# Second normalisation of a gated cross-attention and mixture-of-experts block: scale and bias on ScalarE in place of a two-scalar operation on VectorE

## The chip, the cores and the metric

The kernel runs on one core of a Trainium2 chip. The metric is the time of one execution on the device in microseconds (us). Timed runs give a median; one more execution was recorded by the hardware profiler, and every row below comes from that recording. Engines are named as the profile names them: PE is TensorE (PEld its weight loads), DVE is VectorE, ACT is ScalarE, POOL is GpSimd, SP is SyncE, which here only issues DMAs; SPq, POOLq and so on are the engines' queues.

## The reference: what is computed

There are four sequences (B = 4) of 512 tokens with 512 channels. Each passes a gated cross-attention and then a gated feed-forward part that is a mixture of eight experts (two per token) plus one shared expert:

```python
x = x + jnp.tanh(g_xattn[0]) * xattn(_layernorm(x), ctx_512, Wq, Wkv_expand, Wout)
x = x + jnp.tanh(g_ffn[0])   * ffn(_layernorm(x), gate_w, w1, w2, w3, ws1, ws2, ws3)

def _layernorm(x, axis=-1, eps=1e-05):
    m = jnp.mean(x, axis=axis, keepdims=True)
    v = jnp.var(x, axis=axis, keepdims=True)
    return (x - m) / jnp.sqrt(v + eps)

# ffn: scores = softmax(xf @ gate_w.T); top 2 of 8 experts; y = weighted sum of the
# two chosen experts' outputs; z = silu(xf @ ws1.T) * (xf @ ws3.T) @ ws2.T; y + z
```

The second `_layernorm`, the one ahead of the feed-forward part, is what the change is about.

## The kernel before, in words

The kernel is one program with an instruction list for each engine, written out by hand. Nothing is scheduled by a tool: each engine executes its own list in order, and engines wait for each other on semaphores. A block is one sequence, b = 0 to 3, of four tiles of 128 tokens.

**Blocks.** `iteration(b, prev, nxt)` exists on every engine. It runs the attention of block b, interleaved with `feed_forward(prev)`, the shared expert and the router of the block before. Block 0 is written out, blocks 1 and 2 are a hardware loop, and block 3 (`nxt` false) is written out again. `last_feed_forward` then does the shared expert and the router of block 3. After it comes the expert part: 39 tiles of gathered token rows through the experts' weights, with sums scattered back to the output. That part can begin only when all tokens are routed.

**Products in two halves.** Each f32 operand of a product is held as two f16 parts. ScalarE writes the high part (`turn_hi` for transposed tiles, line 541), VectorE the low part (`turn_lo`, line 815, or 816), and TensorE multiplies three pairs.

**From attention to feed-forward.** For each tile i of block b, VectorE does `make_x1` (line 863, the residual sum into `x_sb`) and `statistics2` (line 831). After tiles 0 and 1, and again after tiles 2 and 3, it does `aggregate2` for the pair p = 0 or 1 (lines 838 and 842, the variance), GpSimd does `power2` (line 415, the inverse root into column 2 of `ln2`), and VectorE does `norm2(b, p)` (line 885): two instructions, each subtracting the mean and multiplying by the inverse root, from `x_sb` into `xn2`. TensorE transposes `xn2` (`turn_x2`, line 1298), ScalarE and VectorE make the halves `x2T`, and `hidden` (line 1343) and `router` use them. SyncE stores `xn2` rows to `xrows` for the expert part.

**Where the two pairs stand.** Pair 0 is normalised at the end of `iteration(b)`, pair 1 at the beginning of the next feed-forward, in `after_attention(f)`. On ScalarE, the places that matter are the end of `iteration` (the scores' copies `scores_out`, line 598, and the softmax's `exps`, line 603; in block 3 instead `split_piece(3)` to `split_piece(7)`), and the beginning of `feed_forward` and `last_feed_forward` (two `turn_hi`, then `exps` or `split_piece(8)`, then `tanh_h`, line 607).

**Weights.** From block 2 on, the eight experts' weights come in 16 pieces. `split_piece(k)` on ScalarE (line 541, 128x1536) writes the high half of piece k and, for pieces whose low half GpSimd makes, a scaled copy back; the low half is then made by GpSimd (line 462, four instructions a piece) or VectorE (line 816). GpSimd's other work is the softmax's subtraction and multiplication (lines 446, 453) and the scatters of token lists (line 432).

The first normalisation already has the form scale and bias on ScalarE: `norm1` (line 573) with `bias1` (line 857) on VectorE.

Of the kernel before, what the change touches and what calls it, by code (L numbers as in the profile page):

```python
# [25 lines left out]
ALU = mybir.AluOpType  # L26
# [44 lines left out]
def block_program(nc, x, ctx_rows, gates, wq, wkv, wout, gate_w, experts, out):  # L71
    with ExitStack() as stack:  # L72
# [129 lines left out]
        y_mm, x1_ready = sem("y_mm"), sem("x1_ready")  # L202
        ln2_step, ln2_stats, xn2_ready = sem("ln2_step"), sem("ln2_stats"), sem("xn2_ready")
        lg_mm, lg_max, lg_out, lg_exp = sem("lg_mm"), sem("lg_max"), sem("lg_out"), sem("lg_exp")
        route_step, mask_ready, pos_mm, route2_step, pos_out, pairs_ready = (sem(n) for n in (
# [333 lines left out]
        def _(act):  # L539
# [60 lines left out]
            def exps(b, i):  # L600
                act.wait_ge(sub_ready, 4 * b + i + 1)
                si = S[:, i * NH * SK:(i + 1) * NH * SK]
                nc.scalar.activation(si, si, ACT.Exp, scale=float(HD) ** -0.5 / (S_Q * S_KV)).then_inc(exp_ready, 1)

            def tanh_h(b, i):
                act.wait_ge(h_mm, 4 * b + i + 1)
                nc.scalar.activation(th[:, i % 2, :], mm_bank[i % 2][:, 0:INTER], ACT.Tanh,
                                     scale=0.5 / (S_LN * S_W)).then_inc(th_ready, 1)
# [14 lines left out]
            def feed_forward(f, nxt):  # L623
# [10 lines left out]
                scores_out(c, 3)  # L634
                turn_hi(c, "x2", 1)
                exps(c, 2)
                tanh_h(f, 0)
# [32 lines left out]
            def last_feed_forward(f):  # L670

                c = f + 1
                turn_hi(c, "x2", 0)
                turn_hi(c, "x2", 1)
                split_piece(8)
                tanh_h(f, 0)
# [21 lines left out]
            def iteration(b, prev, nxt):  # L698
# [22 lines left out]
                if nxt:  # L721
                    scores_out(b + 1, 0)
                    scores_out(b + 1, 1)
                    exps(b + 1, 0)
                    scores_out(b + 1, 2)
                    exps(b + 1, 1)
                else:
                    for k in range(3, 8):
                        split_piece(k)
# [80 lines left out]
        def _(dve):  # L810
# [68 lines left out]

            def norm2(b, p):  # L880
                if not isinstance(b, int) or b > 0:
                    dve.wait_ge(st_rows, 64 * b)
                dve.wait_ge(ln2_power, 2 * b + p + 1)
                for i in (2 * p, 2 * p + 1):
                    V.tensor_scalar(xn2[:, i * D:(i + 1) * D], x_tile(4 * b + i), ln2[:, i, 0:1], ln2[:, i, 2:3],
                                    ALU.subtract, ALU.mult).then_inc(xn2_ready, 1)

# [145 lines left out]
            def after_attention(f):  # L1033
# [6 lines left out]
                turn_lo(c, "x2", 1)  # L1040
                norm2(f, 1)

# [128 lines left out]
            def iteration(b, prev, nxt):  # L1171
# [41 lines left out]
                aggregate2(b, 0)  # L1213
                norm2(b, 0)
                if nxt:
# [410 lines left out]
```

## Time and profile before

| | |
|---|---|
| median of 3 timed runs | 522.28 us (520.1 to 526.24) |
| profiled execution, its own time | 521.47 us |
| span of the profiled execution | 519.7 us |
| mean granted TensorE clock | 0.947 of full speed |
| PE busy | 436.1 us (84%) |
| DVE busy | 318.6 us (61%) |
| ACT busy | 245.8 us (47%) |
| POOL busy | 245.0 us (47%) |

The execution's own time has 1.77 us around the span. Times inside the span are counted from its start. An engine's busy share is an average over stages: the start to about 72 us, four blocks of 56 to 63 us each, the last feed-forward to about 301 us, a gap in which lists and rows are fetched, and the expert part from 316 us. In a timeline row the first number is the start, the second the length from the first start to the last end when several instructions are merged (x2), and the square bracket says how long the engine had been idle before it and what it had waited for.

### The profile page before, as it was taken

The page shows a single profiled execution, that of the slowest core. Times are in us where ns is not written, and L with a number is a line of the kernel's source. Part 1 is how long each engine was busy: PE and PEld are TensorE (multiplying, and loading weights), DVE is VectorE, ACT ScalarE, POOL GpSimd, SP SyncE. Part 2 cuts the span into 40 slices and gives each one's busy share as a digit, 9 for nine tenths or more (in the row PEclk, how much of TensorE's full clock was granted, in tenths as well). Part 3 has the DMA queues.
Part 4 walks back from the last instruction along what each step waited for, and adds up shares of the span by engine and source line. Part 5 has one row for each costly group of instructions (what it writes and reads, how often), then busy time and mean ns, then how long its engine had stood idle before and what let it go on. Part 6 is the DMA issues. An engine that isn't in the chain of part 4 may idle for free. (4 is left out here: it accounts for less than half of the span.)

```text
span 519.7 us, 8145 instructions
## 1 busy us (share of the span) xinstructions
PE 436.1 (84%) x2432; PEld 232.6 (45%) x2433; DVE 318.6 (61%) x641; ACT 245.8 (47%) x425; POOL 245.0 (47%) x209
## 2 busy tenths in 40 slices
PE   2699599988999889987867625999999999999991
PEld 1355355554555545553333202455455545445540
DVE  4798868987588865897988761433433334343330
ACT  4878644663356534485746320343344343434430
POOL 4008325405544154465687813255555555455432
PEclk9999989999999999998978855999999999999997
DMA  8970001120011100325747664266576575655653
GB/s 327 412 304 1 0 1 42 42 81 2 1 64 38 61 0 0 108 116 182 244 121 241 165 122 102 41 109 113 104 121 109 99 119 102 123 105 110 108 75 42
DMA packets 26375, 55.31 MB, mean 106 GB/s; under 512 B 9136, under 2 KB 9264, under 8 KB 25712
## 3 DMA queue, kind: packets, MB, share of 16 engines
q0 software_dynamic: 9760, 20.49, 22.3%
q1 hardware_dynamic: 16592, 34.54, 20.2%
q8 instruction: 11, 0.18, 0.1%
q14 instruction: 12, 0.10, 0.1%
HBM read 31.51 MB, written 23.50 MB: 106 GB/s over the span
## 5 line engine op out<-in xcount | busy, mean ns | idle before, releaser
L1293 PE MATMUL bank<-arena 128*128 128x512 f16 (+1 forms) x576 | 109.5, 347 | 3.2 <-issue 1.5
L1293 PE MATMUL bank<-arena,GT 128*128 x468 | 109.6, 385 | 0.1
L526 POOL DMA_INDIRECT out<-Y,entry x39 | 61.6, 1579 | 84.4 <-ACT Y L792 39.0
L1293 PE MATMUL bank<-arena,gT 128*128 (+1 forms) x330 | 84.1, 393 | 6.3 <-DVE gT L815 5.8
L1293 PEld LDWEIGHTS bank<-arena 128*128 128x128 f16 x576 | 55.9, 98 | 51.4 <-issue 3.8
L541 ACT ACTIVATE arena<-bank 128x512 f16<-128x512 f32 (+1 forms) x88 | 49.7, 586 | 52.5 <-PE bank L1293 32.3
L1293 PEld LDWEIGHTS bank<-arena,GT 128*128 128x128 f16 x468 | 46.3, 99 | 48.5 <-issue 3.1
L815 DVE TENSOR_TENSOR GT<-bank,GT 128x512 f16<-128x512 f32 x39 | 27.0, 692 | 61.0 <-ACT GT L541 61.0
L453 POOL TENSOR_TENSOR arena<-arena,rd 128x1024 f32<-128x1024 f32 x16 | 30.5, 1905 | 52.3 <-DVE rd L928 52.3
L1293 PEld LDWEIGHTS bank<-arena,gT 128*128 128x128 f16 x330 | 32.7, 100 | 44.7 <-DVE gT L815 5.8
L1293 PE MATMUL bank<-arena,x2T 128*128 128x512 f16 x192 | 47.9, 403 | 4.4 <-DVE x2T L815 4.4
L509 POOL DMA_INDIRECT G<-xrows,entry x39 | 38.8, 996 | 26.5 <-issue 12.6
L1257 DVE SCALAR_TENSOR_TENSOR uu<-th,bank 128x256 f32<-128x256 f32 x39 | 16.4, 421 | 56.3 <-ACT th L777 56.3
L777 ACT ACTIVATE th<-bank 128x256 f32<-128x256 f32 x39 | 15.0, 384 | 69.8 <-PE bank L1293 69.8
L792 ACT ACTIVATE Y<-bank,entry 128x512 f32<-128x512 f32 x39 | 26.8, 688 | 44.7 <-PE bank L1293 44.7
L446 POOL TENSOR_TENSOR arena<-arena,mx 128x1024 f32<-128x1024 f32 x16 | 30.3, 1899 | 26.4 <-DVE mx L917 26.4
L1298 PE MATMUL bank<-ident,G 128*128 128x128 f32 x156 | 25.1, 285 | 19.6 <-DMA G<-xrows,entry 14.8
L432 POOL DMA_INDIRECT lists<-pair,slot x32 | 34.1, 1065 | 13.9 <-issue 13.9
L1298 PE MATMUL bank<-ident,arena 128*128 128x128 f32 x192 | 29.1, 291 | 13.6 <-DVE arena L815 9.5
L815 DVE TENSOR_TENSOR arena<-bank,arena 128x512 f16<-128x512 f32 x48 | 31.3, 684 | 9.8 <-ACT arena L541 9.2
L816 DVE SCALAR_TENSOR_TENSOR arena<-bank,arena 128x512 f16<-128x512 f32 (+1 forms) x40 | 25.8, 654 | 14.0 <-ACT arena L541 13.7
L462 POOL TENSOR_TENSOR arena<-x_sb,arena 128x384 f16<-128x384 f32 x32 | 30.0, 970 | 7.5 <-ACT x_sb L541 7.5
(126 smaller groups left out, 596.2 us busy)
## 6 DMA issues: line engine op xcount, KB each, us to landing
x_sb<-in_experts SPq DMA_DIRECT2D x16, 768.0 KB, 6.1
xrows<-xn SPq DMA_DIRECT2D x16, 256.0 KB, 2.2
out<-x_sb SPq DMA_DIRECT2D x16, 256.0 KB, 2.1
xrows<-Y SPq DMA_DIRECT2D x1, 2304.0 KB, 23.9
out<-Y SPq DMA_DIRECT2D x1, 2304.0 KB, 28.8
x_sb<-in_x SPq DMA_DIRECT2D x2, 1024.0 KB, 7.8
x_sb<-in_x SPq DMA_DIRECT2D x1, 2048.0 KB, 15.8
arena<-in_wq SPq DMA_DIRECT2D x1, 1024.0 KB, 8.0
```

What stands on the lines that cost most here:

```text
L432: nc.gpsimd.indirect_dma_start(out=lists[:, :], out_offset=bass.IndirectOffsetOnAxis(ap=slot[:, i, k:k + 1], axis=0), in_=pair[:, i, k, :] ...
L446: nc.gpsimd.tensor_tensor(sv, sv, mx[:, i, :].unsqueeze(2).to_broadcast([P, NH, SK]), ALU.subtract).then_inc(sub_ready, 1)
L453: nc.gpsimd.tensor_tensor(sv, sv, rd[:, i, :].unsqueeze(2).to_broadcast([P, NH, SK]), ALU.mult).then_inc(p_ready, 1)
L462: nc.gpsimd.tensor_tensor(wlo[:, cols], raw[:, cols], whi[:, cols], ALU.subtract).then_inc(w_split[w_slot(k)], 1)
L509: nc.gpsimd.indirect_dma_start(out=G[:, j % RING, :], out_offset=None, in_=xrows[:, :], in_offset=bass.IndirectOffsetOnAxis(ap=entry[:, j, ...
L526: nc.gpsimd.indirect_dma_start(out=out, out_offset=bass.IndirectOffsetOnAxis(ap=entry[:, j, 0:1], axis=0), in_=Y[:, j % RING, :], in_offse ...
L541: return nc.scalar.activation(dst, src, ACT.Copy, scale=scale)
L792: nc.scalar.activation(Y[:, s, :], e_y[s][:, :], ACT.Copy, scale=entry[:, bass.ds(j, 1), 1:2].rearrange("p n c -> p (n c)").bitcast(F32)). ...
L815: return V.tensor_tensor(dst, src, high, ALU.subtract)
L816: return V.scalar_tensor_tensor(out=dst, in0=src, scalar=scale, in1=high, op0=ALU.mult, op1=ALU.subtract)
L1293: last = nc.tensor.matmul(dst, a, b, start=n == 0, stop=n == len(steps) - 1)
L1298: last = nc.tensor.transpose(dst[:, c * P:(c + 1) * P], src[:, c * P:(c + 1) * P], ident[:, :])
```

## The change

The second normalisation becomes x times scale plus bias on ScalarE. VectorE no longer touches the 128x512 tiles; it makes one small tensor for each pair of tiles, bias = -mean times inverse root (128x2, into column 3 of `ln2`), behind the same wait for GpSimd's power. The new semaphore `ln2_bias` tells ScalarE of it. On ScalarE, `norm2(b, 0)` stands in the lists of blocks 0 to 2 between `scores_out(b + 1, 2)` and `exps(b + 1, 1)`, and in block 3 between `split_piece(5)` and `split_piece(6)`. `norm2(f, 1)` stands behind the second `turn_hi` in both kinds of feed-forward. No other instruction is added or removed, and the queues of SyncE, GpSimd and TensorE are as before.

```diff
+            def norm2(b, p):
+
+                if not isinstance(b, int) or b > 0:
+                    act.wait_ge(st_rows, 64 * b)
+                act.wait_ge(ln2_bias, 2 * b + p + 1)
+                for i in (2 * p, 2 * p + 1):
+                    if not isinstance(b, int):
+                        pass_waits(act)
+                    nc.scalar.activation(xn2[:, i * D:(i + 1) * D], x_tile(4 * b + i), ACT.Identity,
+                                         bias=ln2[:, i, 3:4], scale=ln2[:, i, 2:3]).then_inc(xn2_ready, 1)
+
...
                 turn_hi(c, "x2", 0)
                 scores_out(c, 3)
                 turn_hi(c, "x2", 1)
+                norm2(f, 1)
                 exps(c, 2)
                 tanh_h(f, 0)
...
                 turn_hi(c, "x2", 0)
                 turn_hi(c, "x2", 1)
+                norm2(f, 1)
                 split_piece(8)
                 tanh_h(f, 0)
...
                     scores_out(b + 1, 2)
+                    norm2(b, 0)
                     exps(b + 1, 1)
                 else:
-                    for k in range(3, 8):
+                    for k in range(3, 6):
+                        split_piece(k)
+                    norm2(b, 0)
+                    for k in range(6, 8):
                         split_piece(k)
...
-            def norm2(b, p):
-                if not isinstance(b, int) or b > 0:
-                    dve.wait_ge(st_rows, 64 * b)
+            def bias2(b, p):
+
+                w = ln2[:, 2 * p:2 * p + 2, :]
                 dve.wait_ge(ln2_power, 2 * b + p + 1)
-                for i in (2 * p, 2 * p + 1):
-                    V.tensor_scalar(xn2[:, i * D:(i + 1) * D], x_tile(4 * b + i), ln2[:, i, 0:1], ln2[:, i, 2:3],
-                                    ALU.subtract, ALU.mult).then_inc(xn2_ready, 1)
+                V.scalar_tensor_tensor(out=w[:, :, 3], in0=w[:, :, 0], scalar=-1.0, in1=w[:, :, 2],
+                                       op0=ALU.mult, op1=ALU.mult).then_inc(ln2_bias, 1)
...
                 turn_lo(c, "x2", 1)
-                norm2(f, 1)
+                bias2(f, 1)
...
                 aggregate2(b, 0)
-                norm2(b, 0)
+                bias2(b, 0)
```

Three places show how ScalarE's list moves. The first is the written-out end of block 3 and the beginning of the last feed-forward: `arena<-bank 128x512 x4` are the attention's high halves, `arena<-x_sb` and `x_sb<-x_sb` the pieces 3 to 7, `x2T<-bank` the two `turn_hi`, the next pair piece 8, `th<-bank` the first tanh. Before:

```order
L541 ACTIVATE arena<-bank 128x512 x4
L541 ACTIVATE arena<-x_sb 128x1536 x2
L541 ACTIVATE x_sb<-x_sb 128x1536
L541 ACTIVATE arena<-x_sb 128x1536 x2
L541 ACTIVATE x_sb<-x_sb 128x1536
L541 ACTIVATE arena<-x_sb 128x1536
L541 ACTIVATE x2T<-bank 128x4x128 x2
L541 ACTIVATE arena<-x_sb 128x1536
L541 ACTIVATE x_sb<-x_sb 128x1536
L607 ACTIVATE th<-bank 128x256
```

The same place on ScalarE, from piece 4 on, in the changed kernel:

```order
L542 ACTIVATE x_sb<-x_sb 128x1536
L542 ACTIVATE arena<-x_sb 128x1536
L614 ACTIVATE xn<-x_sb,ln 128x512 x2
L542 ACTIVATE arena<-x_sb 128x1536
L542 ACTIVATE x_sb<-x_sb 128x1536
L542 ACTIVATE arena<-x_sb 128x1536
L542 ACTIVATE x2T<-bank 128x4x128 x2
L614 ACTIVATE xn<-x_sb,ln 128x512 x2
L542 ACTIVATE arena<-x_sb 128x1536
L542 ACTIVATE x_sb<-x_sb 128x1536
L619 ACTIVATE th<-bank 128x256
```

Pair 0 now stands ahead of both instructions of piece 6 and the one of piece 7, which stand ahead of the two `turn_hi`; pair 1 stands ahead of piece 8 and the tanh.

The second place is ScalarE's end of block 0, where the last rows were a scores copy and the second softmax exponential; now the pair stands between them (in blocks 1 and 2 likewise):

```order
L542 ACTIVATE arena<-bank 128x512 x4
L599 ACTIVATE arena<-bank 128x512 x4
L604 ACTIVATE arena<-arena 128x1024
L599 ACTIVATE arena<-bank 128x512 x2
L614 ACTIVATE xn<-x_sb,ln 128x512 x2
L604 ACTIVATE arena<-arena 128x1024
```

The fifth row is new; the rows around it stood in this order before.

The third is VectorE at the end of block 3, after the changed variance step: one small instruction, then the residual sum of tile 2, its statistics, the low half of transposed tile 0 and the residual sum of tile 3, in the changed kernel:

```order
L860 TENSOR_SCALAR ln<-ln 128x2
L902 SCALAR_TENSOR_TENSOR ln<-ln 128x2
L881 SCALAR_TENSOR_TENSOR x_sb<-bank,gl,x_sb 128x512
L849 BN_STATS mv<-x_sb 128x6
L833 TENSOR_TENSOR x2T<-bank,x2T 128x4x128
L881 SCALAR_TENSOR_TENSOR x_sb<-bank,gl,x_sb 128x512
```

Where the second row stands there were two instructions `xn<-x_sb,ln 128x512` before; nothing else moved on VectorE.

## Rows read from the trace of the kernel before

**Rows 1.** Windows: us, busy (count) of each engine, PEclk, DMA share, GB/s.

```profile
135.00:197.50 62.50, 57.92 (x368) 32.55 (x368) 49.14 (x102) 31.52 (x57) 25.56 (x19) 1.00 0.10 34
254.00:301.00 47.00, 34.43 (x187) 16.23 (x186) 39.60 (x84) 24.84 (x28) 38.20 (x38) 0.81 0.57 166
```

**Rows 2.** Timeline of GpSimd in the last feed-forward.

```profile
259.62 3.51 POOL L462 TENSOR_TENSOR arena<-x_sb,arena 128x384 f16<-128x384 f32 x4
...
285.96 1.03 POOL L432 DMA_INDIRECT lists<-pair,slot  x1 [1.35 <-issue]
```

**Rows 3.** Waits of SyncE's queue, 300 to 310 us: us in total, times, longest.

```profile
SPq L366 <- DMA lists<-pair,slot: 2.6, 1, 2.6
```

**Rows 4.** Timeline of VectorE, end of block 3 and last feed-forward.

```profile
259.42 3.74 DVE L842 TENSOR_SCALAR ln<-ln 128x2 f32<-128x2 f32 x1
264.08 1.00 DVE L885 TENSOR_SCALAR xn<-x_sb,ln 128x512 f32<-128x512 f32 x2 [0.92 <-POOL ln L415]
...
266.50 0.67 DVE L815 TENSOR_TENSOR x2T<-bank,x2T 128x512 f16<-128x512 f32 x1
...
270.19 2.12 DVE L885 TENSOR_SCALAR xn<-x_sb,ln 128x512 f32<-128x512 f32 x2 [0.33 <-POOL ln L415]
...
275.40 1.28 DVE L815 TENSOR_TENSOR x2T<-bank,x2T 128x512 f16<-128x512 f32 x2
```

**Rows 5.** Timeline of ScalarE over the same stretch.

```profile
254.17 2.84 ACT L541 ACTIVATE arena<-x_sb 128x1536 f16<-128x1536 f32 x2
256.92 1.47 ACT L541 ACTIVATE x_sb<-x_sb 128x1536 f32<-128x1536 f32 x1
261.89 1.48 ACT L541 ACTIVATE arena<-x_sb 128x1536 f16<-128x1536 f32 x1 [3.51 <-DMA x_sb<-in_experts]
265.43 1.08 ACT L541 ACTIVATE x2T<-bank 128x512 f16<-128x512 f32 x2 [2.06 <-PE bank L1298]
...
272.57 0.39 ACT L607 ACTIVATE th<-bank 128x256 f32<-128x256 f32 x1 [0.30 <-PE bank L1293]
```

**Rows 6.** Small VectorE operations: one source line, then timeline rows with GpSimd's beside.

```profile
L857 DVE SCALAR_TENSOR_TENSOR ln<-ln x3: 162/168/168, 12.7 to 67.5; 128x4 f32<-128x4 f32 x2, 128x8 f32<-128x8 f32 x1
...
245.65 0.93 DVE L968 SCALAR_TENSOR_TENSOR sc<-oh,sc 128x32 f32<-128x32 f32 x1
...
245.62 3.52 POOL L462 TENSOR_TENSOR arena<-x_sb,arena 128x384 f16<-128x384 f32 x4 [5.36 <-ACT x_sb L541]
```

**Rows 7.** Timeline of VectorE, end of block 1 and next feed-forward, GpSimd's row last.

```profile
144.96 2.59 DVE L885 TENSOR_SCALAR xn<-x_sb,ln 128x512 f32 x2 [0.85 <-POOL ln L415]
...
150.75 0.68 DVE L815 TENSOR_TENSOR x2T<-bank,x2T 128x512 f16<-128x512 f32 x1
...
153.57 1.00 DVE L885 TENSOR_SCALAR xn<-x_sb,ln 128x512 f32 x2 [0.33 <-POOL ln L415]
...
144.91 1.89 POOL L446 TENSOR_TENSOR arena<-arena,mx 128x1024 f32<-128x1024 f32 x1
```

**Rows 8.** Timeline of ScalarE over the same stretch.

```profile
146.84 1.06 ACT L603 ACTIVATE arena<-arena 128x1024 f32<-128x1024 f32 x1 [2.05 <-POOL arena L446]
148.72 0.60 ACT L541 ACTIVATE x2T<-bank 128x512 f16<-128x512 f32 x1 [0.83 <-PE bank L1298]
...
154.28 0.39 ACT L607 ACTIVATE th<-bank 128x256 f32<-128x256 f32 x1 [2.22 <-PE bank L1293]
...
159.47 1.51 ACT L573 ACTIVATE arena<-x_sb,ln 128x512 f32 x2
```

**Rows 9.** Timeline of TensorE: the same stretch, then block 2's transposes of pair 1.

```profile
151.49 2.76 PE L1293 MATMUL bank<-arena,x2T 128*128 128x512 f16 x12 [1.05 <-DVE x2T L815]
...
155.19 2.75 PE L1293 MATMUL bank<-arena,x2T 128*128 128x512 f16 x12
...
217.03 1.11 PE L1298 MATMUL bank<-ident,xn 128*128 128x128 f32 x8 [0.24 <-DVE xn L885]
```

## What the change does to the time: the prediction

> **What bounds the kernel now.** The windows view comes first, by stage [rows 1]. In a steady block PE is busy 57.9 of 62.5 us at full clock, DVE 49.1, ACT 31.5: TensorE sets the pace there and has some 4.6 us of waits, so freeing VectorE can return only what lies in those waits. In the last feed-forward (254 to 301 us) PE is busy 34.4 of 47 us, DVE 39.6, POOL 38.2, and the granted clock is 0.81. There no engine is full and a chain through all of them sets the time: normalise, transpose, halves, router, choice of experts, and then GpSimd's scatters, which begin at 285.96 [rows 2]. The expert part waits for those lists, so what this chain loses, the end loses. The timelines of each engine around the eight normalisations, read side by side, give the rest: each engine works its list in order, so for every place I ask what stands behind the new instruction.
>
> **The pieces, priced.** Removed from VectorE: two instructions for each of eight pairs, 1.00 us a pair when undisturbed [rows 4, 7], but 2.59 when GpSimd's softmax instruction is running (it starts at 144.91, the norm at 144.96) [rows 7]. Added to ScalarE: two activations a pair; the first normalisation's pair of the same shape takes 1.51 [rows 8]. Added to VectorE: the bias, 0.17 us by `bias1`'s 162 to 168 ns [rows 6]. Whether the bias is held up by GpSimd, as the old norm was, no row shows for this very instruction. The nearest is the same operation on small SBUF tensors at 245.65: 0.93 us, started 0.03 after a GpSimd instruction [rows 6]. The bounds are 0 and the length of GpSimd's instruction; I take held, since this row has the bias's kind of operands.
>
> The Trainium skill, Perfetto Trace Analysis, section Optimizing Scalar/DVE Operations, says that an operation with a VectorE performance mode is faster there, and that moving it to ScalarE may pay if VectorE is saturated. The trace agrees with its first half (1.00 against 1.51 a pair); for the second half, VectorE is at 79% in a steady block. Taken as a rule against the change, it would add 0.5 us for each pair on the path and no more.
>
> **Blocks 0 to 2 (steady block 1 as the example).** The bias would start where the norm did, 144.96, right behind GpSimd's 1.89 us instruction from 144.91, and end at about 146.85 instead of 147.55. ScalarE, idle there until 146.84 [rows 8], then does the pair to 148.4, the exponential (1.06) to 149.4 and the `turn_hi` (0.60), which before began at 148.72, to 150.0. VectorE's `turn_lo` then starts at 150.1, not 150.75 [rows 7]; by VectorE's own list, 3.2 us from the norm's end to `turn_lo`, it would be 150.05, so both arrive together. Gain so far 0.65, and `hidden(0)` on PE, which had waited 1.05 for it and began at 151.49 [rows 9], begins at 150.85. For pair 1 the bias starts 0.65 before 153.57, at 152.9, with GpSimd idle (its next work waits for VectorE's `head_max`, queued behind the bias), and ends at 153.1; ScalarE's pair ends at 154.6, where VectorE's ended at 154.57. So the transpose of tile 3 and `hidden(1)`, 155.19 before, move by 0.1 at most: the gain is given back, because the slower pair starts earlier and ends at the same time. Behind it ScalarE's exponential and tanh are late: tanh at 155.5, not 154.28 [rows 8], and the two `turn_hi` of tiles 2 and 3 by 1.0. TensorE works on `hidden(1)` until 157.9, and VectorE gets through its queue by 158.0, so this is covered. Result: -0.1 for each of blocks 0 and 1. In block 2 PE did wait 0.24 for VectorE's norm ahead of this pair's transposes [rows 9], so an earlier pair 1 is worth more; there I take -0.4. Sum -0.6; bounds per block -0.65 (nothing given back) and +1.0 (the late `turn_hi` uncovered).
>
> **Block 3, pair 0.** This is the costly place. Piece 5 on ScalarE ends at about 255.6 (half of the pair from 254.17) [rows 5]. Now ScalarE waits there for the bias. The bias needs GpSimd's power, which stands behind its `split_piece(4)`, busy until 263.13 [rows 2]; the norm began at 264.08 [rows 4]. So ScalarE stands for 8.7 us, with pieces 6 and 7 queued behind. Before, these filled that wait: piece 6 until 258.4, piece 7 from 261.89 to 263.37 when its load had landed [rows 5]. Now: bias to 264.25, pair 264.3 to 265.8, piece 6 (1.42 + 1.47, less overlap: 2.8) to 268.5, piece 7 (1.4) to 269.9, and only then `turn_hi` of tile 0, which had begun at 265.43: +4.5. VectorE had come to `turn_lo` of tile 0 at 266.50; the half is now ready at 270.5: +4.0. Behind it on VectorE stand the residual sum of tile 3, its statistics and the variance, so all of pair 1 moves by 4.0.
>
> **Block 3, pair 1.** The bias would start at 270.19 + 4.0 = 274.2. GpSimd's next work is `split_piece(6)`, ready by then, so the bias is held by its first instruction. The norm there took 2.12 against 1.00, a hold of 1.1 [rows 4]; the small operation at 245.65 was held 0.7 [rows 6]. I take 0.8 all told, to 275.0. The upper bound is `L842`, which stood through all four of GpSimd's instructions (3.74 us) [rows 2, 4]. Then the pair to 276.5, piece 8 (2.8, by piece 6) to 279.3, and tanh of tile 0 at 279.3, not 272.57 [rows 5]: +6.7. VectorE had not used the tanh at once: its two `hidden` steps (0.8) ended at 275.4 where `turn_lo` of tiles 2 and 3 began [rows 4], so they began 1.65 after the tanh's end. Now they follow directly: 279.7 + 0.8 = 280.5, +5.1. The router needs that low half of tile 3. From here the chain has the spacing of before: logits, choice, places, scatters, landing, list loads, gather. The late pieces have cover: loads 10 to 15 are each released by splits that move by no more than the chain.
>
> **The sum.** +5.1 in block 3, -0.6 in the others: +4.5. Against the profiled execution's own time, 521.47 + 4.5 = 526.0. That execution lies 0.8 below the median of the timed runs, so I name the time from the median: 522.28 + 4.5 = **526.8 us**. Since the bound for telling a change is about 1% (5.2 us), and the three runs spread from 520.1 to 526.24, this is just within it.
>
> **Rivals.** (B) The bias is so short that GpSimd's instruction doesn't hold it. Then in a block it ends at 145.15, `hidden(0)` is limited by PE's own transposes (about -1.0), and ScalarE's pair 1 ends 0.5 earlier: -0.6, -0.6, -0.9; and block 3 is 0.8 cheaper. +4.3 - 2.1 = +2.2, 524.5. Against it speaks the row at 245.65. (C) Not all of the delay reaches the end. SyncE waited 2.6 us for the last scattered packets to land, after it had issued the last store [rows 3]. Should the stragglers not recur at the new instant, the end has 2.6 less: +1.9, 524.2. For it: every other wait in this tail is of an engine; against it: the stores and the load that share the queues with the scatters move along. (D) The bias of block 3's pair 1 is held through all four of GpSimd's instructions, as `L842` was: 3.5 in place of 0.8, +7.2, 529.5. For it: the same place in GpSimd's list (four in a row, nothing between); against it: the norm that stood in this very place was held by one. The same time results if the late `turn_hi` in the blocks have no cover (+1.0 a block). (E) The other side, **faster**: VectorE bounds the steady blocks, and what it is relieved of comes off in full. It is 3.59 - 0.34 = 3.25 us a block for an unheld bias, -9.7 for three, with block 3 net -4.6, 517.7. It decides from 1.7 a block (5.1 / 3). By the skill's page named above, moving the work pays where VectorE is saturated. Against it: VectorE is idle 13.4 of 62.5 us in a block, and its lead runs into products that are not ready [rows 1].
>
> **How the numbers follow.** Forecast 0.52, B 0.12, C 0.12, D 0.14, E 0.08, anything else 0.02. The range that leaves out E and little of D, with the forecast's own bounds (525.0 to 528.8), is 523.0 to 530.0. Slower by over 1% (over 527.5): nearly all of D and a third of the forecast, 0.31. Faster by over 1% (under 517.1): half of E and the rest, 0.06. Within 1%: 0.63.
>
> **What would show it.** In the changed kernel's trace: ScalarE idle for 8 to 9 us ahead of the first activation into `xn` in block 3, waiting for the bias (the central step); the `turn_hi` of tile 0 there 4 to 5 us later against the start of the block's first residual sum; the scatters of block 3 about 4.5 later than 285.96 in the span's time. In the blocks: bias instructions of 1.9 us for pair 0 and 0.17 for pair 1; the start-to-start spacing of blocks (62.5 us) shorter by about 0.1. The prediction is wrong if that spacing falls by more than 0.5, if the bias of pair 0 is short, or if SyncE's wait for the last scattered packets, 2.6 us before, is gone.

## The result, and the profile after

The changed kernel takes 527.57 us (median of 20 runs, 524.0 to 531.32) beside 525.05 us (20 runs, 519.83 to 528.72) for the kernel before on the same chips: a ratio of 1.0073 with a 95% interval of 1.0045 to 1.0101, so 3.8 us slower (2.4 to 5.3). The time is inside the predicted range. Ratios, here and below, leave out executions over 1.5% above the fastest of their kernel, which are two of e4's twelve (525.63 and 526.80 us; its median below still counts them) and one of the kernel before. The profiled execution has a span of 524.9 us against 519.7. Below, a time "into the block" counts from the start of that block's first residual sum (`make_x1`).

The page's first lines, busy time of each engine:

```profile
span 524.9 us, 8171 instructions
...
PE 434.5 (83%) x2432; PEld 231.1 (44%) x2433; DVE 309.5 (59%) x633; ACT 255.3 (49%) x441; POOL 244.7 (47%) x209
```

VectorE lost 9.1 us of work, ScalarE gained 9.5, and the kernel became slower. The same two windows as in [rows 1]:

```profile
135.00:197.50 62.50, 57.11 (x364) 32.01 (x362) 47.74 (x99) 33.29 (x60) 25.59 (x19) 1.00 0.09 34
254.00:301.00 47.00, 31.38 (x174) 14.62 (x171) 31.08 (x77) 25.85 (x31) 33.94 (x35) 0.79 0.58 166
```

In the last feed-forward every engine but ScalarE does less in 47 us than before (VectorE 31.1 against 39.6: two normalised pairs are gone, the variance step took 0.62 for 3.74, and later work has moved out of the window). The stretch is longer, not fuller. The new ScalarE line and the new VectorE line, by source line:

```profile
L614 ACT ACTIVATE xn<-x_sb,ln x16: 801/809/817, 82.9 to 273.3; 128x512 f32<-128x512 f32 x8, 128x512 f32 x8
...
its engine sat idle before it (us, times) until:
  DVE ln L902: 21.9, 8
```

```profile
L902 DVE SCALAR_TENSOR_TENSOR ln<-ln x8: 164/522/1869, 81.0 to 271.6; 128x2 f32<-128x2 f32 x8
```

ScalarE stood idle for 21.9 us in front of its normalising activations, waiting for the eight biases. Such a wait costs only where something late is queued behind it, and the experiments below show that this is block 3. ScalarE there, to be read beside [rows 5]:

```profile
254.17 1.47 ACT L542 ACTIVATE arena<-x_sb 128x1536 f16<-128x1536 f32 x1
261.86 1.52 ACT L614 ACTIVATE xn<-x_sb,ln 128x512 f32<-128x512 f32 x2 [6.22 <-DVE ln L902]
263.29 1.47 ACT L542 ACTIVATE arena<-x_sb 128x1536 f16<-128x1536 f32 x1
264.66 1.47 ACT L542 ACTIVATE x_sb<-x_sb 128x1536 f32<-128x1536 f32 x1
266.04 1.47 ACT L542 ACTIVATE arena<-x_sb 128x1536 f16<-128x1536 f32 x1
267.41 1.06 ACT L542 ACTIVATE x2T<-bank 128x512 f16<-128x512 f32 x2
272.62 1.52 ACT L614 ACTIVATE xn<-x_sb,ln 128x512 f32<-128x512 f32 x2 [4.16 <-DVE ln L902]
274.05 1.47 ACT L542 ACTIVATE arena<-x_sb 128x1536 f16<-128x1536 f32 x1
275.42 1.47 ACT L542 ACTIVATE x_sb<-x_sb 128x1536 f32<-128x1536 f32 x1
276.80 0.37 ACT L619 ACTIVATE th<-bank 128x256 f32<-128x256 f32 x1
```

Pieces 6 and 7 (263.29 to 267.4) run behind the pair, with the two `turn_hi` straight behind them; piece 8 (274.05) and the tanh follow pair 1 in the same way. VectorE, to be read beside [rows 4]:

```profile
255.74 1.76 DVE L834 SCALAR_TENSOR_TENSOR arena<-x_sb,arena 128x1536 f16<-128x1536 f32 x1 [2.04 <-ACT arena L542]
257.41 0.74 DVE L881 SCALAR_TENSOR_TENSOR x_sb<-bank,gl,x_sb 128x512 f32<-128x512 f32 x1
...
259.42 0.62 DVE L860 TENSOR_SCALAR ln<-ln 128x2 f32<-128x2 f32 x1
261.60 0.16 DVE L902 SCALAR_TENSOR_TENSOR ln<-ln 128x2 f32<-128x2 f32 x1 [1.56 <-POOL ln L416]
...
268.02 0.69 DVE L833 TENSOR_TENSOR x2T<-bank,x2T 128x512 f16<-128x512 f32 x1 [4.75 <-ACT x2T L542]
...
271.65 0.88 DVE L902 SCALAR_TENSOR_TENSOR ln<-ln 128x2 f32<-128x2 f32 x1 [0.25 <-POOL ln L416]
...
277.99 1.28 DVE L833 TENSOR_TENSOR x2T<-bank,x2T 128x512 f16<-128x512 f32 x2
```

VectorE, relieved of the normalisation, waits 4.75 us for ScalarE's high half. GpSimd's timeline there, where the power of pair 0 now comes at 260.84 (before: behind its split from 259.62, [rows 2]) and the scatters of block 3 at 288.56 (before 285.96):

```profile
256.67 4.21 POOL L463 TENSOR_TENSOR arena<-x_sb,arena 128x384 f16<-128x384 f32 x4
260.84 0.73 POOL L416 TENSOR_TENSOR ln<-ln,minus_half 128x2 f32<-128x2 f32 x1
...
288.56 1.03 POOL L433 DMA_INDIRECT lists<-pair,slot  x1 [1.35 <-issue]
```

And SyncE's wait for the last scattered packets, 2.6 in [rows 3]:

```profile
SPq L367 <- DMA lists<-pair,slot: 4.9, 1, 4.9
```

The difference of the spans, 5.2 us, put together from the traces' milestones (us; "first residual sum" is `make_x1` of tile 0):

| stretch | before | after | difference |
|---|---|---|---|
| start to block 0's first residual sum | 75.30 | 74.13 | -1.17 |
| to block 3's first residual sum | 178.85 | 177.98 | -0.87 |
| tile 0's to tile 1's residual sum, block 3 | 3.26 | 5.30 | +2.04 |
| to the first scatter of block 3 | 28.55 | 31.15 | +2.60 |
| to the last scatter | 9.91 | 9.93 | +0.02 |
| to the first load of a list | 12.18 | 14.49 | +2.31 |
| to the first gather | 4.32 | 3.76 | -0.56 |
| to the end of the span | 207.33 | 208.16 | +0.83 |

The first row lies ahead of the first changed instruction (the bias at 81.0) and differs between executions by as much (74.1 to 76.2 in the kernels below, 78.4 in e4). Rows two to four give +3.77, beside 3.8 in the timed runs, but they aren't the change's work alone, and that they agree so closely is in part chance. Row two holds two things that come and go between profiles of kernels with the same work there: a stop of TensorE of 1.21 us at 197.58, and a fall of TensorE's granted clock that before has in block 2 and after hasn't (1.6 us). Without both it is about -0.4. Row three is block 2's gain given back at a load (3.47 us in e6, which changes block 3 alone, and 5.28 in e7, which doesn't change it). The last rows of the span, +2.31 at the landing above all, are left to the part on rival C.

A steady block's pair 0 and pair 1 in block 1, first on ScalarE, to be read beside [rows 7, 8]:

```profile
145.82 1.52 ACT L614 ACTIVATE xn<-x_sb,ln 128x512 f32 x2 [2.24 <-DVE ln L902]
...
148.20 0.58 ACT L542 ACTIVATE x2T<-bank 128x512 f16<-128x512 f32 x1
...
151.90 1.52 ACT L614 ACTIVATE xn<-x_sb,ln 128x512 f32 x2 [1.68 <-DVE ln L902]
...
154.28 0.36 ACT L619 ACTIVATE th<-bank 128x256 f32<-128x256 f32 x1
```

VectorE's two biases there, the first behind GpSimd's softmax instruction, the second free:

```profile
143.75 1.87 DVE L902 SCALAR_TENSOR_TENSOR ln<-ln 128x2 f32<-128x2 f32 x1 [0.84 <-POOL ln L416]
...
151.51 0.16 DVE L902 SCALAR_TENSOR_TENSOR ln<-ln 128x2 f32<-128x2 f32 x1 [0.19 <-POOL ln L416]
```

TensorE's `hidden(0)` and the transposes ahead of `hidden(1)`, to be read beside [rows 9]:

```profile
149.55 2.76 PE L1310 MATMUL bank<-arena,x2T 128*128 128x512 f16 x12 [0.26 <-DVE x2T L833]
152.77 1.43 PE L1315 MATMUL bank<-ident,xn 128*128 128x128 f32 x8 [0.45 <-ACT xn L614]
154.04 2.32 PE L1310 MATMUL bank<-arena,x2T 128*128 128x512 f16 x10
```

Into the block, `hidden(0)` begins at 12.74 (before 151.49 - 138.02 = 13.47), 0.73 earlier, and `hidden(1)` at 17.23 (before 17.17): the gain is given back within one block. TensorE's wait moved from 1.05 ahead of `hidden(0)` to 0.45 ahead of the last transpose, whose releaser is now ScalarE's pair.

### The profile page after: what moved, and what is told of

It reads as the page before. It is cut to its first block and busy times, and to the rows that moved or that the text cites. A ratio compares the mean times of both kernels' runs of the same rounds, so it can differ in the third digit from the quotient of the medians.

```text
span 524.9 us, 8171 instructions
## 1 busy us (share of the span) xinstructions
PE 434.5 (83%) x2432; PEld 231.1 (44%) x2433; DVE 309.5 (59%) x633; ACT 255.3 (49%) x441; POOL 244.7 (47%) x209
## 3 DMA queue, kind: packets, MB, share of 16 engines
q0 software_dynamic: 9760, 20.49, 21.9%
## 5 line engine op out<-in xcount | busy, mean ns | idle before, releaser
L1310 PE MATMUL bank<-arena,gT 128*128 (+1 forms) x330 | 82.5, 387 | 6.3 <-DVE gT L833 5.8
L1315 PEld LDWEIGHTS bank<-ident,G 128*128 128x128 f32 x156 | 18.8, 145 | 34.9 <-issue 30.9
```

Of the source, the lines that this page charges most:

```text
L1310: last = nc.tensor.matmul(dst, a, b, start=n == 0, stop=n == len(steps) - 1)
L1315: last = nc.tensor.transpose(dst[:, c * P:(c + 1) * P], src[:, c * P:(c + 1) * P], ident[:, :])
```

## The experiments

All eleven kernels carry two small edits beside the one named: GpSimd's loads of the numbers that its adds wait for assert the numbers' bounds, and ahead of the expert part TensorE waits for all pieces of a round where it waited for those of one expert. E1 is the kernel before with these edits alone, e2 the changed kernel with them; every other experiment is to be read against these two. Each was timed in five rounds. The columns are the ratio to the kernel before on the same chip, and three lengths from the profiled execution: from block 0's to block 3's first residual sum, from there to the first scatter of block 3, and SyncE's wait for the last scattered packets.

| kernel | median, us | ratio (95%) | blocks 0-2 | to scatter | landing wait |
|---|---|---|---|---|---|
| before | | | 178.85 | 31.81 | 2.6 |
| after | 527.57 | 1.0073 (1.0045 to 1.0101) | 177.98 | 36.45 | 4.9 |
| e1 before | 520.72 | 0.9973 (0.9950 to 0.9996) | 180.49 | 31.36 | 2.5 |
| e2 after | 527.33 | 1.0097 (1.0064 to 1.0131) | 178.01 | 36.48 | 3.4 |
| e3 pair 0 behind pieces | 523.30 | 1.0012 (0.9986 to 1.0038) | 181.14 | 33.54 | 2.1 |
| e4 both behind pieces | 521.40 | 0.9964 (0.9929 to 0.9999) | | | |
| e5 blocks 0-2 only | 522.82 | 1.0001 (0.9970 to 1.0032) | 177.89 | 32.46 | 4.3 |
| e6 block 3 only | 526.73 | 1.0074 (1.0037 to 1.0111) | 178.77 | 36.98 | 4.4 |
| e7 pair 0 of 0-2 only | 519.39 | 0.9937 (0.9901 to 0.9973) | 174.55 | 31.42 | 4.3 |
| e8 e4, stores first | 522.48 | 1.0000 (0.9970 to 1.0029) | 176.99 | 32.90 | 4.0 |
| e9 e1, stores first | 522.44 | 0.9985 (0.9949 to 1.0020) | 178.87 | 32.14 | 3.8 |
| e10 e7, stores first | 519.35 | 0.9927 (0.9896 to 0.9959) | 176.03 | 32.15 | 5.2 |
| e11 pair 0 of all | 521.63 | 0.9972 (0.9938 to 1.0006) | 174.61 | 33.26 | 6.0 |

E4's lengths are left out of the table: its profiled execution took 525.63 us, 4.2 more than its median. In the profiles of after and of e1 to e4, TensorE stands still once at the end of block 1, for 1.2 us (after, e2, e4), 1.9 (e1) and 2.6 (e3); in those of before and of e5 to e11 it doesn't. Kernels with the normalisation on either engine are on both sides, so it isn't the change; what causes it isn't shown. In e3 the granted clock fell behind that stop (0.57 from 200 to 204 us, 1.00 there in e1). So block 1 was longer than before's 62.56 by 1.1 us in after, e2 and e4, by 1.8 in e1 and by 4.3 in e3, which the fourth column includes. As the level of "VectorE everywhere" I take the mean of e1 and e9, 0.9979. E1 to e4 ran on one chip, e5 to e8 on a second and e9 to e11 on a third, so e5 to e8 have no such kernel on their own chip.

**E1 and e2, the two controls.** E1's edit to the waits, in short (that to the bounds is left out here):

```diff
-pe.wait_ge(w_split[w_slot(k)], PARTS * (w_round(k) - 1) + (e + 2) // E * PARTS)
+pe.wait_ge(w_split[w_slot(k)], PARTS * w_round(k))
```

> The kernel before, with the two small edits that every kernel of this study carries: GpSimd's queue asserts the bounds of the value that each add of rows waits for, and TensorE waits for all of the last four weight pieces ahead of the first expert product, in place of a wait that depends on the tile's expert. It is the zero point of the others. Both theories: the pieces were ready 7 us before that product, and GpSimd waits for others in the expert part, so +0.0 us against the kernel before, within 1.0. More than +2 would mean that the assertion is on the path, and then the others are to be read against this one.

> The changed kernel with the same two edits. Both theories: +3.8 us against the kernel before (2.4 to 5.3), and as much against e1. In its trace ScalarE idles about 6 us ahead of the first normalising activation of block 3.

Measured: 0.9973 and 1.0097. The loss by the change is 6.2 us against the mean of e1 and e9 (0.0118 of 522.4), more than the 3.8 of the unedited pair, though the intervals overlap. Against e1 alone, the comparison that was forecast, it is 6.5 us where 3.8 was expected. E1 itself came out 1.4 us below the kernel before, where 0.0 within 1.0 was expected. All comparisons below are among kernels with the edits.

**E5 and e6, one part of the change each.** A selector sends a pair to ScalarE or leaves it on VectorE; in e5 all blocks but block 3 use ScalarE, in e6 block 3 alone.

```diff
+def by_scalar(b, p):
+    return not (isinstance(b, int) and b == B - 1)   # e5
+    return isinstance(b, int) and b == B - 1         # e6
```

> Scale and bias on ScalarE for blocks 0 to 2 only; both pairs of block 3 are normalised by VectorE as before. Theory Q (all of the loss is ScalarE's queue in block 3): no loss; from the residual sum of block 2 to that of block 3 it is 2 us shorter than in e1, as in e2 (51.6 for 53.4), but tile 1 of block 3 waits for weight pieces 4 and 5, so that at most 0.7 arrives: -0.7 to 0 us against e1. Rival S (ScalarE's late exponential and tanh cost in the blocks): +1 to +3 against e1.

> Scale and bias on ScalarE for block 3 only; blocks 0 to 2 are normalised by VectorE as before. Theory Q, as the prediction's own term for block 3: ScalarE waits 8.5 us ahead of pair 0, the scatters of block 3 start 4 to 5 us later from the block's first residual sum, +5 us against e1. Rival S: +3 or less.

Measured: 1.0001 and 1.0074. Against 0.9979 the blocks cost +0.0022 and block 3 +0.0095, together 0.0117, where e2 shows 0.0118. Each ratio is uncertain by some 0.3%, so the parts add up within that, and the loss is block 3's (+5.0 us). E5 missed its expectation, -0.7 to 0 us against e1: it is 1.5 us above e1 and 1.2 above 0.9979, by its number within the rival's +1 to +3. The times don't decide, since the intervals overlap. The trace speaks against the rival: from block 0's first residual sum to block 3's first scatter e5 has 210.35 us, where e9 has 211.01.

ScalarE in e6:

```profile
264.96 1.52 ACT L620 ACTIVATE xn<-x_sb,ln 128x512 f32<-128x512 f32 x2 [8.62 <-DVE ln L918]
...
270.51 1.05 ACT L547 ACTIVATE x2T<-bank 128x512 f16<-128x512 f32 x2
275.71 1.52 ACT L620 ACTIVATE xn<-x_sb,ln 128x512 f32<-128x512 f32 x2 [4.15 <-DVE ln L918]
...
279.88 0.36 ACT L625 ACTIVATE th<-bank 128x256 f32<-128x256 f32 x1
```

With blocks 0 to 2 as before, ScalarE stands idle for 8.62 us. Into the block (which begins at 254.65) the `turn_hi` comes at 15.86, before at 11.28 (+4.6); the tanh at 25.23, before at 18.42 (+6.8); the first scatter at 36.98, before at 31.81 (+5.2).

**E3 and e4, the same work at another place in ScalarE's list.**

```diff
 else:
-    for k in range(3, 6):
-        split_piece(k)
-    norm2(b, 0)
-    for k in range(6, 8):
+    for k in range(3, 8):
         split_piece(k)
+    norm2(b, 0)
```

and in e4 also, in `last_feed_forward`:

```diff
-norm2(f, 1)
 split_piece(8)
+norm2(f, 1)
 tanh_h(f, 0)
```

> The changed kernel with one thing moved: on ScalarE in block 3, the normalisation of pair 0 stands behind pieces 6 and 7 and not ahead of them. Theory Q (the loss is ScalarE's queue in block 3: pieces 6 and 7 held behind the wait for the bias): the pieces fill the wait again, turn_hi of tile 0 is back at the time of before or 0.5 earlier, pair 1 still costs up to 0.1 at the router, so 0 to +1 us against e1, some 3 less than e2. Theory R (the loss is elsewhere: in the landing of the scattered lists and the expert part, or in the blocks): the same as e2, +3.8.

> As e3, and in the last feed-forward pair 1's normalisation stands behind piece 8 on ScalarE, not ahead of it. Theory Q: piece 8 fills the wait for pair 1's bias as well, tanh of tile 0 comes at most 0.8 us later than before, which VectorE had not waited for, and the last low half comes 0.8 earlier: the scatters of block 3 start 0.5 to 1 us earlier than in e1, and the time is -1 to 0 us against e1. Theory R: as e2, +3.8.

Measured: 1.0012 and 0.9964, against 1.0097 with pair 0 ahead of pieces 6 and 7. The same instructions on the same engine, two pieces further down in its list, give back 4.4 us, of which 2.9 can be seen in the trace ahead of the first scatter (33.54 for 36.48). So most of the loss was not the price of ScalarE's pair but of what stood behind its wait. E3 is still 2.0 us above e1, where 0 to 1 was expected; its clock fall in block 1 is one possible reason, and whether the timed runs had it isn't known.

That pair 1 behind piece 8 gives back more isn't shown. By the ratios e4 has 2.5 us less than e3, but the intervals overlap, and e8, which keeps e4's order, is timed at 1.0000. In e4's own profile the first scatter comes 33.61 us into block 3, as in e3. What e4 and e8 do show is that with both pairs behind the pieces no loss is left that could be measured.

In e3 the pieces run through, and nothing waits for pair 0's bias:

```profile
260.67 1.49 ACT L541 ACTIVATE arena<-x_sb 128x1536 f16<-128x1536 f32 x1 [0.89 <-DMA x_sb<-in_experts]
...
265.56 1.49 ACT L541 ACTIVATE arena<-x_sb 128x1536 f16<-128x1536 f32 x1 [2.03 <-DMA x_sb<-in_experts]
266.95 1.51 ACT L613 ACTIVATE xn<-x_sb,ln 128x512 f32<-128x512 f32 x2
268.55 0.60 ACT L541 ACTIVATE x2T<-bank 128x512 f16<-128x512 f32 x1
```

**E7, only the pair that gains.** Pair 0 of blocks 0 to 2 on ScalarE, pair 1 and block 3 on VectorE:

```diff
 def by_scalar(b, p):
-    return not (isinstance(b, int) and b == B - 1)
+    return p == 0 and not (isinstance(b, int) and b == B - 1)
```

> In blocks 0 to 2, pair 0 on ScalarE and pair 1 on VectorE as before; block 3 on VectorE. Theory G (in a block, the gain of 0.6 at the first hidden product is given back because ScalarE's pair 1 takes 1.5 us where VectorE's takes 1.0, with the exponential behind it): the second hidden product keeps the gain, the blocks are 0.5 to 0.7 shorter start to start than in e1 and e5, -1.5 us against e1. Rival: the spacing of the blocks is set elsewhere, and it reads as e5.

Measured: 0.9937, 1.9 us less than e1. The spacings of the blocks' first residual sums are 61.88, 61.79 and 50.88 us, where the kernel before has 62.72, 62.56 and 53.57; of the last difference, 2.69, some 1.3 to 1.6 is the clock (see block 2 below). In block 1 VectorE's pair 1 comes earlier and TensorE has no wait left ahead of `hidden(1)`:

```profile
150.76 2.76 PE L1326 MATMUL bank<-arena,x2T 128*128 128x512 f16 x12 [0.29 <-DVE x2T L839]
153.45 1.19 PE L1331 MATMUL bank<-ident,xn 128*128 128x128 f32 x8
154.47 2.75 PE L1326 MATMUL bank<-arena,x2T 128*128 128x512 f16 x12
```

The gain of 0.7 us at `hidden(0)` is kept: 0.8 a block. E7 and e5 differ in blocks 0 to 2 in pair 1 alone, and e5's first spacing is 62.65: this is the direct evidence that pair 1 on ScalarE gave the gain back.

**E11, pair 0 of all four blocks, in block 3 behind the pieces.**

```diff
 def by_scalar(b, p):
-    return p == 0 and not (isinstance(b, int) and b == B - 1)
+    return p == 0
```

> Pair 0 of all four blocks on ScalarE, in block 3 behind pieces 3 to 7; pair 1 of all on VectorE. Against the kernel with pair 0 of blocks 0 to 2 alone at 0.9937, block 3's pair 0 costs 0.5 us more by ScalarE's longer pair, and VectorE is free for the residual sum of tile 2 one us earlier, which has to wait for TensorE anyhow: 0.994 to 0.996. If ScalarE's list is at all late there (turn_hi behind the pair), up to 1.5 us more: 0.997. If instead it is VectorE that block 3's chain waits for, as its 3.7 us held variance step may hint, it gains 1 us: 0.992.

Measured: 0.9972, and 1.8 us more to the first scatter than e7 (33.26 against 31.42). By its number it fits the middle case of the expectation, but the trace gives only part of it to ScalarE's list: pair 0 starts 0.44 us after its bias has ended, behind piece 7, and takes 0.5 longer than on VectorE, while GpSimd's power had come 1.07 later into the block than in e7 (9.77 for 8.70). In time e11 isn't told apart from e7, since the intervals overlap.

**E8, e9 and e10, the place of a load.** In the traces of after, e2, e3, e5 and e7, tile 1's residual sum in block 3 comes 5.3 to 5.5 us after tile 0's, before 3.3. In the rows of after above, VectorE's split at 255.74 waits 2.04 for ScalarE, and ScalarE waited 2.07 us at 251.40 for the load of a weight piece, which SyncE issues when block 2's stores to the output base have landed. These three kernels let the stores go ahead of the load of the fourth piece:

```diff
-load_pieces(2, 4)
+load_pieces(2, 3)
 store_base(B - 2, 1, PER)
+load_pieces(3, 4)
```

> As e4, and SyncE issues block 2's last three base stores ahead of the load of weight piece 3, not behind it. In e4 the residual sum of tile 1 in block 3 came 5.3 us after that of tile 0, in e1 4.0: it waits for piece 5, whose load waits for these stores to land. Theory D (the 1.9 us that the blocks gain are given back at this load): the stores land 2 to 3 us earlier, tile 1 follows at 3.3 to 4 us, and 1 to 2 us arrive at the end, -1.5 us against e4. Rival: tile 1 waits for something else, no change against e4, or piece 3 itself is now late, +1.

> The kernel before (VectorE's norms everywhere) with SyncE's list changed in one place: block 2's last stores to the output base stand ahead of the load of the fourth weight piece. If the 1.9 to 2.0 us by which tile 1's residual sum of block 3 comes later after a quicker block 2 hangs on that load's place in the queue, this kernel has the first residual sums of block 3 at most 3.3 us apart as before and changes nothing else: 0 to -1 us. If the place of the stores is worth something by itself (the scatters' tail), it shows here as well: -1 to -3 us. Rival: the four loads queued behind then come later and the split of the fourth piece with them: +1 to +2 us.

> Pair 0 of blocks 0 to 2 on ScalarE, everything else on VectorE, and the base stores ahead of the load of the fourth piece. The same kernel without the reordered stores was 0.9937 of before. If the load of pieces behind those stores takes part of block 2's gain, this one keeps it: 1 to 1.5 us less than that kernel, 0.991. If the distance between the residual sums is set otherwise, no difference from 0.994.

Measured: the two residual sums are 3.69, 3.60 and 3.59 us apart in e8, e9 and e10 (e7, without the reordering, 5.28), so the link with the load is real. ScalarE's wait for that load in e8:

```profile
249.46 1.48 ACT L542 ACTIVATE arena<-x_sb 128x1536 f16<-128x1536 f32 x1 [0.45 <-DMA x_sb<-in_experts]
```

But in time it brings nothing: 1.0000 against e4's 0.9964 (1.5 us less had been expected), 0.9985 against e1's 0.9973 (0 to 1 us less expected), 0.9927 against e7's 0.9937, with overlapping intervals in each pair. In e10 the way from block 3's first residual sum to its first scatter isn't shorter than in e7 (32.15 against 31.42). The theory that this distance costs the end its 2 us has fallen. The traces show what ends last there instead. GpSimd in e10:

```profile
254.38 2.20 POOL L440 DMA_INDIRECT lists<-pair,slot  x1 [0.31 <-issue]
...
257.86 3.51 POOL L470 TENSOR_TENSOR arena<-x_sb,arena 128x384 f16<-128x384 f32 x4
261.48 0.73 POOL L423 TENSOR_TENSOR ln<-ln,minus_half 128x2 f32<-128x2 f32 x1
```

The normalisation of pair 0 waits for the power at 261.48, which is 9.41 us into the block; in e7 it comes at 8.70. Tile 1 is earlier in e10, but GpSimd isn't: one of block 2's scatters took 2.20 us beside VectorE's split of 1.76 us that had started at 253.98 (0.96 in e7, where it had started first), and the four split instructions and the power stand behind it.

**Which version is best.** E7 and e10 are both below the kernel before by more than their intervals (3.3 and 3.8 us). Taken together, 0.9932, against e1 and e9 together, 0.9979, it is 0.5% or 2.5 us, with an uncertainty of some 0.3%. So of the 3.6 us some 2.5 belong to moving pair 0 of blocks 0 to 2. The rest would belong to the edits that all these kernels carry; that these gain 1.1 us isn't shown, since e9's interval includes 1.

## Why the prediction held, point by point

**The time.** Forecast +4.5 us, measured +3.8 (2.4 to 5.3); 526.8 against 527.57, with the kernel before at 525.05 in those runs where its median had been 522.28. That the time itself came within 0.8 us is luck: the starting point was 2.8 too low and the change 0.7 too high. The forecast's own bounds, 525.0 to 528.8, follow from no term that it gives; its bounds per block lead to 525.4 and 530.4.

**The prices of the instructions** held: ScalarE's pair 1.52 for 1.51, VectorE's bias 0.16 when free for 0.17. The choice whether GpSimd holds the bias up came out as taken: 1.87 us for pair 0 (predicted 1.9), 0.88 for pair 1 of block 3 (predicted 0.8). So rival B, a bias too short to be held, is refuted by its own row. Rival D, a bias held through four instructions, is refuted by the 0.88; its second form, late `turn_hi` without cover in the blocks, by the spacing of blocks 0 and 1, 62.68 against 62.72.

**Blocks 0 and 1, -0.1 each.** Spacing -0.04 from block 0 to 1, `hidden(0)` 0.73 earlier (predicted 0.65), `hidden(1)` 0.06 later. E7 confirms by the opposite test that pair 1 on ScalarE gives it back. From block 1 to 2 the spacing is 63.69 against 62.56, by the stop of 1.21 us at 197.58; e5, with the same instructions there and no stop, has 62.54.

**Block 2, -0.4, held, and a clock came on top.** The spacing from block 2 to 3 fell by 1.96 (53.57 to 51.61). The change's own part is where TensorE's 2.35 us wait ends, 34.80 us into the block for 35.17: 0.37 earlier. From there to the end of its next long wait it is 6.67 us in after and 8.27 in before, and this 1.60 isn't the change's own work. TensorE's granted clock, windows of the kernel before and of after:

```profile
234.00:238.00 4.00, 2.25 (x7) 1.11 (x8) 3.13 (x6) 1.76 (x4) 3.60 (x4) 0.70 0.64 187
238.00:242.00 4.00, 4.00 (x25) 2.65 (x23) 1.84 (x3) 1.39 (x3) 2.26 (x3) 0.87 0.35 45
```

```profile
234.00:238.00 4.00, 2.69 (x18) 1.92 (x19) 2.69 (x6) 1.82 (x5) 3.60 (x4) 1.00 0.64 197
238.00:242.00 4.00, 2.14 (x15) 1.24 (x14) 3.89 (x7) 2.92 (x5) 1.83 (x3) 1.00 0.34 31
```

In the kernel before the granted clock fell from 2.4 to 1.2 GHz for part of these windows, and six matmuls at 236.21 took 2.77 us where the same six take 1.46; in after it didn't fall. E1, e6 and e9 (VectorE in block 2) show the fall, after, e2, e3, e4, e5, e7, e8 and e11 don't. E10 shows that this is a thing apart from the normalisation: it has e7's instructions there, the clock fell (0.65 and 0.92 in these windows), and its spacing is 52.32 against e7's 50.88. The same stretch is 8.00 us in e10 and 6.66 in e7. So the fall costs 1.3 to 1.6, and the rest is the predicted 0.4. (E5, at 52.70 without a fall, has tile 1's residual sum of block 2 1.1 us later after tile 0's than before; why isn't shown.) The prediction had no term for the clock: a fall in the kernel after and none in before would have moved the result by as much the other way.

**Block 3, pair 0, +4.5 at `turn_hi`.** E6, where nothing ahead of block 3 differs, shows each number of this step: ScalarE stands 8.62 (predicted 8.7), `turn_hi` +4.6 (4.5). In the changed kernel itself it stood 6.22. There piece 5 ended later into the block, behind the load that piece 4 had waited for (2.07 at 251.40), and the power came a little earlier, 8.73 into the block for 9.1. So `turn_hi` was +4.0 there: 0.6 less than in e6, whose power came at 9.30.

**Block 3, pair 1, +5.1 at the scatters.** E6: tanh +6.8 (predicted 6.7), scatters +5.2. In after: +6.3 and +4.6. The timed runs agree: +5.0 us for e6 against the mean of e1 and e9. E3 confirms the cause for pair 0, the pieces queued behind the wait, by removing it. For pair 1 alone the experiments don't: e4 and e3 aren't told apart.

**The sum.** -0.87 and +4.64 to the first scatter in the traces, where I had -0.6 and +5.1. The -0.87 is made of -0.4 of the change's own, +1.1 of the stop at 197.58 and -1.6 of the clock, so its nearness to -0.6 is luck. The +4.64 is 0.5 below e6's +5.2, by the power that came 0.6 earlier into the block.

**The signs.** Of what the prediction said would show it, `turn_hi` (+4.0), the two lengths of the bias and the spacing of the steady blocks came. ScalarE's idle time of 8 to 9 us came in e6 alone (6.22 in the changed kernel), and the scatters began 2.6 us after 285.96, not 4.5, since the whole profile of after lay 2.0 us ahead at block 3's first residual sum.

**Rival C**, stragglers gone, went the other way: SyncE's landing wait is 4.9, not 0. I had said that the prediction would be wrong if that wait vanished; I hadn't allowed for its growth. Over the twelve profiles without e4 it lies between 2.1 and 6.0. It doesn't follow the change, since e5 and e7, with VectorE in block 3, have 4.3, and it doesn't follow when the scatters come: e7, e10 and e11, which scatter early, have 4.3 to 6.0, but e6 and after, which scatter latest, 4.4 and 4.9. In all twelve SyncE issues its last store 18.4 us after the first scatter of block 3, so the wait is in how long the scatters take to land. A store issued 8.9 us after that first scatter lands late in the same profiles (17.3 us after it in e3, which waits 2.1, and 23.8 in e11, which waits 6.0); that other transfers of this stretch slow both is a rival that no run tests. It can hide a gain or a loss: e11 reaches its first scatter 3.1 us sooner than e9 (207.87 against 211.01, counted from block 0's first residual sum, some 1.3 to 1.6 of it the clock), stands 2.2 us longer for the landing, and is timed 0.7 us faster, which isn't told apart from nothing. What sets the landing wasn't settled.

**Rival E**, VectorE bounds the steady blocks: refuted by e5, in which VectorE is relieved in three blocks and the time is 1.0001. It needed 1.7 us a block. With the bias held at 1.87 and free at 0.16, VectorE was in fact relieved of 1.56 a block (3.59 before), and the most that any kernel got is e7's 0.8. The Trainium skill, Perfetto Trace Analysis, section Optimizing Scalar/DVE Operations, says that moving work to ScalarE may make sense where VectorE is saturated. In a steady block VectorE was busy 79%; no run here shows what a fuller VectorE would make of it.

## What to carry to other kernels

Moving an operation to an idler engine moves its wait as well: price the instructions queued behind that wait on the new engine before the operation itself. Here block 3's two pairs in front of weight pieces, where ScalarE stood 8.6 and 4.2 us, cost 5 us, and behind the pieces the same instructions cost nothing that could be measured. And move only the instances that gain: of eight pairs three were worth it, measured together in e7, those that VectorE did while GpSimd held it up.

## What the runs showed of the hardware

A small VectorE instruction that starts as GpSimd works can last as long as GpSimd's instruction: the 128x2 bias took 1.87 us beside GpSimd's 1.89 and 0.16 alone. It goes the other way too: a scatter of GpSimd took 2.20 us in e10 beside a VectorE split of 1.76 that had started 0.40 ahead of it, and 0.96 in e7, where the scatter had started first.

How long VectorE is held by a series of four GpSimd instructions differs. The variance step (`L842`, in after `L860`) was held 3.74 us in the kernel before, to the end of the whole series, having started 0.20 ahead of it (259.42 and 259.62) [rows 2, 4]; in e6, e8, e9 and e10 it was the same. In after it took 0.62, having started 0.32 into the third instruction, and ended with that one; in e2, e3, e4, e5 and e7 it was the same. The bias of pair 1, started 0.05 into a series' first instruction (271.65 and 271.60), took 0.88, one instruction. But starting inside a series is no protection. In e1 the step started 0.21 into the second of the four and was held to the end of the fourth, and in e11 likewise:

```profile
262.10 2.48 DVE L841 TENSOR_SCALAR ln<-ln 128x2 f32<-128x2 f32 x1
...
261.02 3.53 POOL L462 TENSOR_TENSOR arena<-x_sb,arena 128x384 f16<-128x384 f32 x4
```

What decides between one instruction and the rest of the series isn't shown.

TensorE's granted clock fell to half for part of 234 to 242 us in five profiles (before, e1, e6, e9, e10) and not in the other eight. E7 and e10 are on different sides and differ only in the order of two of SyncE's entries; in before and after alike TensorE had been idle 2.35 us just ahead. What decides it stayed open, and it is worth 1.3 to 1.6 us here, more than the change is worth in any single block but block 3.
